# A fused cross-attention kernel: two of four probability tiles of the packed steps turned by VectorE and transfers in place of TensorE

## The reference

```
q = (layernorm(x) @ Wq).reshape(B, Sq, H, D)      # H = 16, D = 128
k, v = (ctx @ Wk), (ctx @ Wv)                     # in heads as well
q, k = rmsnorm(q, gq), rmsnorm(k, gk)
attn = softmax(einsum('bqhd,bkhd->bhqk', q, k) * D ** -0.5)
out  = einsum('bhqk,bkhd->bqhd', attn, v).reshape(B, Sq, H * D) @ Wo
```

## Time and profile before

| | |
|---|---|
| median of 3 runs | 1465.05 us (1462.61 to 1465.51) |
| profiled execution: span | 1461.5 us (the page gives no other time of it) |
| busy: TensorE, VectorE, ScalarE, GpSimd | 1437.8, 1107.0, 977.5, 864.5 us |
| moved by DMA | 142.74 MB, 98 GB/s over the span |
| packed steps | about 486 to 1216 us |

### The profile page before, as it was taken

The page is one execution under the profiler, slowest core; times in us unless marked ns, Lnnn a source line. Parts: engine busy times, 40 slices in busy tenths (PEclk is TensorE's granted clock), DMA queues, the critical chain, the costliest instruction groups (busy, mean ns, idle before and its releaser), DMA issues.

```text
span 1461.5 us, 23763 instructions
## 1 busy us (share of the span) xinstructions
PE 1437.8 (98%) x8086; PEld 1223.0 (84%) x8086; DVE 1107.0 (76%) x2100; ACT 977.5 (67%) x2224; POOL 864.5 (59%) x701
## 2 busy tenths in 40 slices
PE   8999999999999999999999999999999999999998
PEld 6778788888888888888888888888888888888887
DVE  7888777777777777777777777777777776787777
ACT  7864477777776667667676767667676765666664
POOL 4785555555554566666575757575666655664341
PEclk9999999999999999999999999999999999999999
DMA  8420011111111333434333433433434331321002
GB/s 325 159 66 16 22 44 45 57 44 44 44 44 44 139 124 126 149 108 147 124 129 127 139 123 127 139 117 132 136 115 144 125 126 36 107 82 37 8 1 87
DMA packets 55495, 142.74 MB, mean 98 GB/s; under 512 B 5392, under 2 KB 5392, under 8 KB 55376
## 3 DMA queue, kind: packets, MB, share of 16 engines
q1 hardware_dynamic: 51616, 128.90, 26.1%
q0 software_dynamic: 3760, 12.32, 3.0%
HBM read 126.79 MB, written 14.42 MB: 97 GB/s over the span
## 4 chain that ended last, share of the span: by engine, by line
PE 82%; DVE 7%; ACT 4%; POOL 4%; issue 2%; DMA 0%; ACTq 0%; SPq 0%; DVEq 0%; POOLq 0%
PE w_bank L505 10%; PE w_bank L507 10%; PE w_bank L506 10%; PE j_bank L505 9%; PE j_bank L507 9%; PE j_bank L506 9%; PE t_bank L573 7%; PE s_bank L505 4%; PE s_bank L507 4%; PE s_bank L506 4%; PE t_bank L538 2%; POOL q_scale L1855 2%; POOL wo_lo L1815 2%; ACT prob L927 1%; PE t_bank L657 1%
## 5 line engine op out<-in xcount | busy, mean ns | idle before, releaser
L927 ACT ACTIVATE prob<-s_bank,neg_bias,q_scale 128x512 f32<-128x512 f32 x255 | 198.0, 777 | 186.5 <-DVE neg_bias L1422 186.4
L1262 DVE TENSOR_TENSOR probT_lo<-t_bank,probT_hi 128x512 fp32r<-128x512 f32 x260 | 176.4, 689 | 168.4 <-ACT probT_hi L892 168.4
L1476 DVE SCALAR_TENSOR_TENSOR x_sb<-w_bank,inv_sum,x_sb 128x512 f32<-128x512 f32 x254 | 188.4, 744 | 0.0
L1401 DVE TENSOR_REDUCE neg_max<-s_bank 128x1 f32<-128x512 f32 x255 | 168.6, 682 | 0.9 <-PE s_bank L507 0.9
L1815 POOL TENSOR_TENSOR xnT_lo<-xnT_raw,xnT_hi 128x512 fp32r<-128x512 f32 (+2 forms) x47 | 126.5, 2693 | 61.5 <-ACT xnT_hi L892 61.5
L573 PE MATMUL t_bank<-ident,prob 128*128 128x128 f32 x1008 | 151.4, 273 | 1.3 <-ACT prob L927 1.1
L892 ACT CAST probT_hi<-t_bank 128x512 fp32r<-128x512 f32 x260 | 150.1, 590 | 1.8 <-PE t_bank L515 1.8
L1855 POOL TENSOR_TENSOR q_scale<-q_ss,minus_half 128x4 f32<-128x4 f32 x64 | 65.9, 1030 | 143.6 <-DVE q_ss L1414 143.6
L505 PE MATMUL j_bank<-wkv_lo,cT_hi 128*128 128x256 f32 x512 | 145.1, 283 | 0.7 <-DVE oT_lo L1262 0.4
L507 PE MATMUL j_bank<-wkv_hi,cT_lo 128*128 128x256 f32 x512 | 144.6, 282 | 0.0
L506 PE MATMUL j_bank<-wkv_hi,cT_hi 128*128 128x256 f32 x512 | 144.4, 282 | 0.0
(11 more groups left out here) (308 smaller groups left out, 4454.2 us busy)
## 6 DMA issues: line engine op xcount, KB each, us to landing
stage<-w SPq DMA_DIRECT2D x96, 256.0 KB, 3.4
xnT_raw<-w_gu SPq DMA_DIRECT2D x31, 704.0 KB, 4.8
cT_raw<-w_gu SPq DMA_DIRECT2D x31, 704.0 KB, 4.7
xnT_raw<-w_dn SPq DMA_DIRECT2D x16, 768.0 KB, 4.4
cT_raw<-w_dn SPq DMA_DIRECT2D x15, 768.0 KB, 4.7
planes<-bits SPq DMA_DIRECT2D x16, 512.0 KB, 4.8
y<-stage SPq DMA_DIRECT2D x31, 256.0 KB, 4.0
x_sb<-x SPq DMA_DIRECT2D x5, 1024.0 KB, 10.9
```

Source lines behind the costliest of these rows:

```text
L927: nc.scalar.activation(prob[:, i, :], score_bank(t, i)[:], ACT.Exp, bias=neg_bias[:, u % 2, i:i + 1], scale=q_scale[:, u % 2, i:i + 1], ac ...
L1262: return nc.vector.tensor_tensor(dst, src, hi, ALU.subtract)
L1401: nc.vector.tensor_reduce(neg_max[:, u % 2, i:i + 1], score_bank(t, i)[:], AX_X, ALU.max, negate=True).then_inc(own_max, 1)
L1476: nc.vector.scalar_tensor_tensor(out=here, in0=w_bank[0][:] if packed else out_bank(t, i)[:], scalar=inv_sum[:, w % 2, i:i + 1], in1=here, ...
```

## The change

For the items whose score step is packed (`moved(u)`, 31 items), probability tiles 0 and 1 no longer go through TensorE. softmax writes them with their columns rearranged in groups of 32; VectorE transposes both tiles in place in blocks of 32x32 (turn_quads, one instruction of 128x1024); SyncE stores the pair to DRAM (512 KB) and loads it back by four transfers of 32 partitions each, which put the blocks in their places; ScalarE makes the high part (moved_hi, 128x1024) and GpSimd, in the next step, the low part (moved_lo, 128x1024). values() waits for that as well. Tiles 2 and 3 are turned as before. The layout of probT becomes tile by tile with runs of 32, for all steps. SyncE's wait for the store stands ahead of the down weights' load, the four loads behind it. On VectorE squares_out moves ahead of rows_to_lo and copy_y.

```diff
+def moved(u):
+    return 0 <= u < NI and T0 <= u + 1 < T0 + NB
+def turned_tiles(u):
+    return (2, 3) if moved(u) else range(NT)
...
+            def store_pair(u):
+                if not moved(u):
+                    return
+                sp.wait_ge(p_quads, MOVES[u] + 1)
+                wait(sp, p_moved, 16 * NT * MOVES[u])
+                sp.dma_start(turn_dram.rearrange("i p m -> p i m"), prob_pair).then_inc(p_stored, 16)
+
+            def load_pair(u):
+                if not moved(u):
+                    return
+                sp.wait_ge(p_stored, 16 * (MOVES[u] + 1))
+                for c in range(NT):
+                    sp.dma_start(prob[c * QUAD:(c + 1) * QUAD, 0:2, :].rearrange("a i (r m) -> a (i r) m", r=NT),
+                                 turn_dram.rearrange("i (r a) (c m) -> c a (i r) m", r=NT, c=NT)[c]).then_inc(p_moved, 16)
...
+                store_pair(t - 1)
                 if 0 <= b < NB:
                     down_weights(b, e)
+                load_pair(t - 1)
...
                 def probs(i):                                   # TensorE
                     if not score:
                         return
+                    if i not in turned_tiles(u):
+                        return
...
                 def values():
                     if not value:
                         return
-                    need(pe, p_lo, 4, w, 4)
+                    wait(pe, p_lo, TILES[w + 1])
+                    wait(pe, pair_lo, MOVES[w + 1])
...
-                        last = product(j_bank[0][:], [a[:, w % 2, 1, j * P:(j + 1) * P] for a in kv],
-                                       [a[:, j, :] for a in probT], j == 0, j == NT - 1)
+                        last = product(j_bank[0][:].rearrange("p (q c) -> p q c", c=QUAD),
+                                       [a[:, w % 2, 1, j * P:(j + 1) * P] for a in kv],
+                                       [a[:, j] for a in probT_keys], j == 0, j == NT - 1)
...
+                def moved_hi():                                 # ScalarE
+                    if not moved(u):
+                        return
+                    act.wait_ge(p_moved, 16 * NT * (MOVES[u] + 1))
+                    need(act, pv_mm, 1, w, 1)
+                    copy_hi(probT_pair(0), prob_pair).then_inc(pair_hi, 1)
...
                     inner_hi()
+                moved_hi()
                 query_squares()
                 probs_hi(3)
...
+                def turn_quads():                               # VectorE
+                    if not moved(u):
+                        return
+                    need(dve, p_exp, 4, u, 2)
+                    flat_pair = prob_pair.rearrange("p i s -> p (i s)")
+                    nc.vector.transpose(flat_pair, flat_pair).then_inc(p_quads, 1)
...
                     gate_up_lo()
+                    squares_out()
                     rows_to_lo()
                     copy_y()
-                    squares_out()
...
                 if packed:
+                    turn_quads()
                     inner(0)
-                    probs_lo(0)
...
-                    probs_lo(1)
...
+                def moved_lo(v):                                # GpSimd
+                    if not moved(v):
+                        return
+                    pool.wait_ge(pair_hi, MOVES[v] + 1)
+                    lower(probT_pair(1), prob_pair, f32(probT_pair(0))).then_inc(pair_lo, 1)
...
                 if up:
                     take_rows(b + 1)
+                moved_lo(w)
                 query_scale()
```

More of the change, by code:

```diff
@@ L123, with flamingo_kernel @@
 LAST = {b: max(t for t in range(NI) if ITEMS[t][1] == b) for b in range(B)}
-def flamingo_kernel(nc, x, xT, ctxT, vecs, w0, bits, w1, w_gu, w_dn, topk_idx, topk_w, x0_dram, rows_dram, y_dram, out):
+QUAD = 32
+def moved(u):
+    return 0 <= u < NI and T0 <= u + 1 < T0 + NB
+def turned_tiles(u):
+    return (2, 3) if moved(u) else range(NT)
+TILES = [sum(len(turned_tiles(v)) for v in range(u)) for u in range(NI + 1)]
+MOVES = [sum(moved(v) for v in range(u)) for u in range(NI + 1)]
+def flamingo_kernel(nc, x, xT, ctxT, vecs, w0, bits, w1, w_gu, w_dn, topk_idx, topk_w, x0_dram, rows_dram, y_dram, turn_dram, out):
     x_tiles = x.rearrange("(b i p) d -> b p i d", b=B, p=P)
@@ L204, in flamingo_kernel, with probT_tile, probT_pair @@
         block_expert = sb("block_expert", [P, NBW], I32)
+        probT_keys = [t[:, :, :].rearrange("p i s -> p (i s)").rearrange("p (q j c) -> p j q c", j=NT, c=QUAD)
+                      for t in probT]
+        def probT_tile(part, i):
+            return probT[part][:, i, :].rearrange("p (r j c) -> p j r c", j=NT, c=QUAD)
+        def probT_pair(part):
+            return probT[part][:, 0:2, :]
+        prob_pair = prob[:, 0:2, :]
         def squares(t):
@@ L534, in turn_keys @@
                     need(pe, q_ss_out, 1, 0, 1)
+                elif moved(t - 1):
+                    need(pe, q_ss_out, 1, t - 1, 1)
                 elif t:
-                    need(pe, p_lo, 4, t - 1, 2)
+                    wait(pe, p_lo, TILES[t - 1] + 2)
                 for j in range(NT):
@@ L569, in probs @@
                         need(pe, p_lo, 4, u, (0, None, 0, 1)[i])
+                    elif moved(u):
+                        wait(pe, p_lo, TILES[u] + i - 2)
                     elif t != LAST_SCORES:
-                        need(pe, p_lo, 4, u, (0, None, 1, 3)[i])
+                        wait(pe, p_lo, TILES[u] + (0, None, 1, 3)[i])
                     for j in range(4):
@@ L661, in table @@
                     pe.wait_ge(place_ready, 1 + NT)
-                    need(pe, p_lo, 4, 0, 4)
+                    wait(pe, p_lo, TILES[1])
                     for c in range(PAIRS):
@@ L925, in softmax @@
                     need(act, s_max, 4, u, i + 1)
-                    need(act, p_turned, 4, u - 1, i + 1)
-                    nc.scalar.activation(prob[:, i, :], score_bank(t, i)[:], ACT.Exp,
+                    if i in turned_tiles(u - 1):
+                        wait(act, p_turned, TILES[max(u - 1, 0)] + list(turned_tiles(u - 1)).index(i) + 1 if u else 0)
+                    else:
+                        wait(act, pair_lo, MOVES[u])
+                    dst, src = prob[:, i, :], score_bank(t, i)[:]
+                    if i not in turned_tiles(u):
+                        dst = dst.rearrange("p (r j c) -> p j r c", j=NT, c=QUAD)
+                        src = bank_keys(score_bank(t, i))
+                    nc.scalar.activation(dst, src, ACT.Exp,
                                          bias=neg_bias[:, u % 2, i:i + 1], scale=q_scale[:, u % 2, i:i + 1],
@@ L933, in probs_hi @@
                         return
[L934 to L936 removed]
+                    if i not in turned_tiles(u):
+                        return
+                    wait(act, p_turned, TILES[u] + list(turned_tiles(u)).index(i) + 1)
+                    copy_hi(probT_tile(0, i), bank_keys(prob_bank(t, i))).then_inc(p_hi, 1)
+                def moved_hi():
[4 more added lines that the diff above has]
+                    copy_hi(probT_pair(0), prob_pair).then_inc(pair_hi, 1)
                 def values_hi():
@@ L1446, in probs_lo @@
                         return
-                    need(dve, p_hi, 4, u, i + 1)
-                    hi, lo = [a[:, :, i * P:(i + 1) * P] for a in probT]
-                    lower(lo, prob_bank(t, i)[:].rearrange("p (j q) -> p j q", j=4), f32(hi)).then_inc(p_lo, 1)
+                    if i not in turned_tiles(u):
+                        return
+                    wait(dve, p_hi, TILES[u] + list(turned_tiles(u)).index(i) + 1)
+                    lower(probT_tile(1, i), bank_keys(prob_bank(t, i)), f32(probT_tile(0, i))).then_inc(p_lo, 1)
+                def turn_quads():
+                    if not moved(u):
+                        return
+                    need(dve, p_exp, 4, u, 2)
+                    flat_pair = prob_pair.rearrange("p i s -> p (i s)")
+                    nc.vector.transpose(flat_pair, flat_pair).then_inc(p_quads, 1)
                 def values_rows():
@@ L2066 @@
     x0 = nc.dram_tensor("x0", (S, D), F32, kind="Internal").ap()
-    flamingo_kernel(nc, *args, x0, rows, y, out)
+    turn = nc.dram_tensor("turn", (2, P, S), F32, kind="Internal").ap()
+    flamingo_kernel(nc, *args, x0, rows, y, turn, out)
     result = run_bass_kernel_spmd(nc, [arrays], core_ids=[0])
```

17 lines of the change are left out of this document (10 added, 7 removed).

## The result

The changed kernel takes 1571.07 us (median of 4 runs, 1568.2 to 1577.02), the kernel before 1465.28 beside it on the same chip: a ratio of 1.0731, 95% interval 1.0706 to 1.0755. It is 7% slower, 106 us; 1593 had been forecast. The profiled execution has a span of 1566.4 us, 104.9 more than before.

The account below looks back on a forecast made before the run. TensorE was taken as the bound, 729.4 of 730 us busy in packed steps. Span 1461.5 - 27.3 (transposes) + 117.5 (stalls) + 37.5 (clock) = 1589.2 us, so 1593 us as median; range 1535 to 1650.

Parts of the forecast that it names:

- The stall: TensorE waits for moved_lo ahead of values(): 20 steps of 3.5 us, 10 of 4.65, one of 0.95, 117.5 us.
- So moved_lo runs 704.86 to 707.27: GpSimd's moved_lo waits for VectorE's gate and up weights' subtraction, so values() starts at 707.3, not 703.78: 3.5 us.
- the shift: moved_hi ahead of query_squares on ScalarE makes sqs_hi, xn and what hangs on them on GpSimd and VectorE 0.58 us late.
- no exclusion: Rival: the VectorE and GpSimd subtractions don't exclude each other here; 20 stalls of 2.2 us, 1552 us; 10%.
- The clock: TensorE's clock falls behind 25 of the 30 long stalls ahead of values(), 1.5 us each: 37.5 us.
- the clock stays up: Rival: TensorE's clock stays up through stalls of 3.5 us and more: 1555 us; 17%.
- The transposes: Two groups of four transposes leave TensorE in each packed step: 0.88 us a step, 27.3 us gained over 31.
- I give it nothing: On VectorE, squares_out ahead of rows_to_lo and copy_y brings q_ss about 1.2 us forward; priced at 0.
- down_hi slips by 0 to 1 us ... so 0: Store's wait on SyncE delays the down weights' load; turn_inner on TensorE comes near the step's end, so cost 0.
- The layout: values() reads runs of 32 elements in all steps: cost 0, far bound 18 us.
- the rival of late loads: The pair's loads land 1 to 2 us late for moved_hi, adding as much stall each step: 1624 to 1655 us; 18%.
- The faster rival: moved_lo is hidden ahead of values() and the 27 us of transposes stay whole: 1438 us; 8%.

Follow-up runs that it names:

- e2: Changed kernel with moved_lo at the end of the step that makes the tiles, ahead of squares_lo: 1488.92 us.
- e1: Changed kernel with the down weights' load issued on SyncE ahead of the store's wait: 1573.67 us.
- e6: Changed kernel with values() running its eight products with the high part first and only then waiting for moved_lo: 1542.80 us.
- e7: Changed kernel with 15 extra matmuls, results overwritten, in front of the wait for moved_lo in new-head steps only: 1551.02 us.
- e3: Changed kernel with both the edits of e1 and e2: 1480.49 us.
- e13: e3 with moved_lo on 2 x 8 columns only, the rest of the pair's low part left out: 0.27%, 4 us, faster than the kernel before.
- e12: Changed kernel with e1's edit and moved_lo given to VectorE instead of GpSimd: 1464.70 us, the kernel before 1465.39 beside it.
- e5: Kernel before with the new layout of probT alone, no tile moved and VectorE's order as before: 1469.47 us.
- e9: Changed kernel with moved_lo ahead of the gather instead of behind it: 1523.75 us.

## Why the prediction was right, and where it was off

- **The mechanism holds**: TensorE waits in front of values() for moved_lo in the steps t = 21 to 49, and longer where a head is new. e2 shows it by moving one call: stall 73.4 to 1.0 us. It is 29 steps and not 31: t = 50 has no gather ahead of moved_lo and stalls for 0.4 us, though it was counted with 3.5, and t = 51 waits no longer than before the change.
- **The stall was mis-sized**: 72.4 us in place of 117.5. The new-head step was near (4.0 measured, 4.65 forecast); the plain one was 1.6 and not 3.5. The step that failed is "So moved_lo runs 704.86 to 707.27": I had VectorE's 128x1408 first and GpSimd second, because it starts sooner. It does start sooner in the record (813.75 against 814.04), in all 19 plain steps with a gather, and yet moved_lo went first in each and VectorE's operation ended 1.5 us after it. 1.3 us of the error are this order. Why GpSimd kept its turn is not shown: the running gather alone does not hold VectorE, whose operation took 1.62 us beside it when nothing of GpSimd's came behind the earlier trace rows. Where VectorE starts *ahead* of the gather, as at 785, the order is the forecast one. The rest of the error is the shift: squares_lo was to come 0.58 us later against scores(0) and came 0.2 sooner (811.51 - 810.56 = 0.95 against 1.15). TensorE's new waits behind its query seem to have given ScalarE the time for moved_hi: in e1, where these waits are gone, squares_lo comes at 1.6 to 2.0 and the plain stalls are 2.1 to 2.5. The rival "no exclusion" had a similar stall, 2.2, for the wrong reason: the exclusion is there, and its price is paid by VectorE and by who waits for it (e6).
- **The clock**: 10 falls, not 25, and 18.6 us in place of 37.5; the plain stalls stayed below the 2.10 us of the earlier trace rows. For each fall 1.5 us was forecast, 1.9 us measured (4.78 against 2.92). The rival "the clock stays up" is refuted by these falls, and e7 shows that the idle time makes them.
- **The transposes** left TensorE as forecast, 0.88 us a step: in e3 the rest of a step that follows a new head's is 15.34 us, 16.26 less 0.92. But "A microsecond of TensorE work removed there shortens the kernel" does not follow from a busy share: e13 keeps 4 of 27 us. A stretch that is 99.9% busy tells that nothing else is late there, not how near other engines are to being late, and the change itself made VectorE later (e12).
- **squares_out forward: "I give it nothing"** looked at what it brings and not at inverses(), which fell behind it. What it may have cost is said at e12, and stays open.
- **"down_hi slips by 0 to 1 us ... so 0"** was the zero that failed. In the trace ScalarE waits up to 1.8 us for the down load in each step, 37.8 us in all, and behind it stand the copies that I had named. e1, in which that wait is gone, has 30.5 us less of rest. I had named the queue and left it unpriced. Together with some 5 us of other waits it more than cancelled the transposes' 27.3 us. So my sum, 23 us too high against the measured 105, hides errors of 45 and 19 us upward against 35 and 6 (values(), beside the falls) downward: that it came so near is in part luck.
- **The layout** cost 0.12 us a step, 5 us in all (e5), not 0, and far from the bound of 18.
- **Transfers**: 3.2 us for the store and 3.5 for a load, where 5.0 and 3.4 had been taken. These are the rows of the page's DMA issues that answer to the earlier trace rows; moved_hi waits for no transfer, so the rival of late loads is out:

```profile
turn<-prob SPq DMA_DIRECT2D x31, 512.0 KB, 3.2
prob<-turn SPq DMA_DIRECT2D x124, 128.0 KB, 3.5
```

- **VectorE's turn** took 1.25 us (1.18 estimated) and fell where it was put:

```profile
823.18 1.25 DVE L1535 STREAM_TRANSPOSE prob<-prob 128x1024 f32<-128x1024 f32 x1 [1.57 <-ACT prob L996]
```

- **The faster rival** (moved_lo hidden, 1438) asked for moved_lo to be done in time, and the stall of 72.4 us says that it was not. e13 grants that and more, and is at 1460: with VectorE's order as in the change the 27 us do not stay whole either.

## What to carry to other kernels

Work taken off the busiest engine pays only as far as no other engine is late in its place; before building, take the same instructions out and put nothing in their place, and see what is left to win. No run here did just that: e13, the nearest, keeps the turn, the copy, the transfers and the new order on VectorE, and keeps 4 us of 27. An instruction moved forward moves others back: look at what falls behind it, and at what the other engine does at that moment, even for an operation of 0.23 us. When a step gives work to a second engine, look for the instruction that wants its result, not for that engine's idle time, and put it where the queue has room ahead of that point (e2, one call moved, won 82 us). A wait put in front of a load in a DMA queue delays that load and all that it feeds; and a load moved away can uncover the next one in the queue (e1).

## What the runs showed of the hardware

- GpSimd and VectorE, each with inputs in SBUF, exclude each other over whole instructions, and who goes first can be GpSimd's subtraction although VectorE's record starts 0.3 us sooner: so in 19 of 19 steps of the changed kernel in which a gather was running on GpSimd at that moment. Where a subtraction was running instead, VectorE went first (e9 at 768.65, e3's 128x1408 ahead of wkv_lo). The Trainium skill ("SBUF — State Buffer", SBUF: two separate sides) has the pair of ports go to whichever operation starts first; the ends in the trace (816.42, then 817.91) agree with a lock, the recorded starts alone (813.75 and 814.04) would give the wrong order. A record of 4.16 us for work of 1.6 to 1.8 is how such a wait looks.
- The same holds for a gather issued on GpSimd: 1.05 us alone, 2.24 beside VectorE's 128x1408. It holds for small operations too: VectorE's inv_sum of 128x4 takes 0.23 us, and 1.12 or 2.10 where a GpSimd subtraction is in the way.
- TensorE's clock: none of 18 idle times of 1.55 to 1.7 us brought a fall in the changed kernel, nor two of 2.0, while in e7 one of 2.0 did; in e6 5 of 10 of 2.0 to 2.2; in e1 10 of 18 between 2.1 and 2.5; in e9 2 of 10 of 2.9; in the changed kernel all 10 of 4.0. The length of the wait alone does not decide.
- With 3.56 us of throwaway matmuls in the wait the clock stays up in all ten steps (e7).
